# Two-layer f32 network, one core: stack constants by DMA, first passes before second passes, and short rounds spread over block 7

## The chip, the cores and the metric

The kernel runs on one core of a Trainium2 chip (trn2). The metric is the device time of one execution in microseconds (us), lower is better; the runs of the kernel before have a median of 3712.45 us.

## What is computed

The reference takes x (4 x 1024 x 128, f32) through two layers. Each layer is four steps of the form x = x + f(layernorm(x)): an attention, a mixture of experts, a second attention, a mixture of experts. Three pieces matter here.

The first attention of layer 0 has 16 heads of 8 values per sequence. Its scores are a causal table of distances (made from the mean of the inputs, through softmax, top-k and a sum of sines), plus one term for each query, one for each key, plus a small product of projected queries and keys:

```python
scores = jnp.take(causal_kern, jnp.maximum(doff, 0), axis=-1)
scores = scores + qm[..., :, None] + km[..., None, :]
scores = scores + MIX * jnp.einsum('bhic,bhjc->bhij', qc, kc) / math.sqrt(CR)
scores = jnp.where(causal, scores, -1000000000.0)
attn = jax.nn.softmax(scores, axis=-1)
```

The second attention of layer 1, the last attention of the network, has 16 heads of 64 values and one common key and value head:

```python
sim = jnp.einsum('bhid,bjd->bhij', q, k)
sim = sim + jnp.transpose(bias, (2, 0, 1))[None] * bias_scale
sim = jnp.where(causal_mask[None, None], -neg, sim)
attn = jax.nn.softmax(sim, axis=-1)
out = jnp.einsum('bhij,bjd->bhid', attn, v)
return out.transpose(0, 2, 1, 3).reshape(b, n, INNER) @ Wout + bout
```

## The kernel before

x stays in SBUF from start to end; the stages run one after another, each a block in which the five engines run programs of their own, coupled by semaphores. SyncE (SP) issues all DMAs.

**`l0a_project` (L1423, to about 119 us).** It normalizes x, transposes it and projects it to the dot parts of queries and keys, in eight groups g of 512 positions (batch b, half `par`). Each part is split into three bf16 pieces (`part["q"]`, `part["k"]`, `part["m"]`, two buffers by `par`) and SP sends them to DRAM (`send_parts` L1010 and L1484; `sent[par]`). ScalarE writes a buffer again two groups later and waits for `sent[par]` first (before L1567). Before the loop SP loads this stage's weights and those of the next mixture of experts (`load_l0_ffn`, L134).

**`l0a_table` (L1613).** It makes the distance table of the first attention. VectorE computes the mixing weights in a chain of small instructions on `l0at_gl`, `l0at_soft`, `l0at_hard` (L1732 to L1748); the sines and products follow from them. At the same time POOL prepares the stacks `l0a_qs` and `l0a_ks`: 128 rows x 3 stacks x 4 heads x 1024, bf16, 24 KB a row. A stack is what TensorE contracts over: rows 0 to 47 dot parts, 48 to 53 single terms and constants, from `MAX_ROWS` = 96 the rows of row maxima; all others have to be zero. POOL fills rows 32 to 63 and 64 to 127 with zeros (L1690, L1692), then SP, after `zeroed`, writes the constant rows (3 DMAs) and loads the dot parts (30 DMAs, `load_stack`, L1023 and L1025).

**`attention_two_pass` (from 277.9 to 874.2 us).** 64 heads in 16 quads. For a quad, `first_pass` (18 tiles t; L1191, L1198) computes scores by queries into `pP`, of which VectorE takes the minima (`low`, L1345); these go back as rows of the stack. `second_pass` (n, 36 units a quad, nine groups of four; L1228, L1231) computes the scores by keys into `pS`, a ring of three; ScalarE takes their exponential (L1317) and POOL multiplies it by the table (L1174), but for one unit in four (`ADDED`), where VectorE adds the table (L1339) and ScalarE takes the exponential after it (L1298). `weigh` (L1245) multiplies with the values. The first passes of a quad are issued `AHEAD` = 20 units before its second passes, one at every even n. The order on TensorE is that of the loop at L1259:

```python
for n in range(N):
    if n + RING - 1 < N:
        second_pass(n + RING - 1)
    if n % 2 == 0:
        quad, t = (n + AHEAD) // STEPS + 1, (n + AHEAD) % STEPS // 2
        if quad < QUADS:
            first_pass(quad, t)
```

**`attention_strips` (tag `l1ba`, from 2582 to 3447 us).** The last attention. A round r is 8 heads by one block of 128 queries; a group is the eight blocks 7, 6, ... 0 of one batch and one half of the heads, 64 rounds in 8 groups. The causal width is 128 keys for block 0, 1024 for block 7. A round is cut into units (one head each for blocks 7 to 4, two for 3 and 2, four for 1, eight for 0), numbered n; `FIRST[r]` is the first unit of round r. For each unit TensorE computes scores into `pS` (`scores`, L2463, or L2458 in block 0), VectorE adds the bias table `tab` and takes the minimum (`lows`, L2575), ScalarE the exponential (`exps`, L2523), VectorE, two units later, transposes in squares of 32 into `pT[r % 2]` (`turn`, L2584). `weigh` (L2483) multiplies the turned weights of a round with the values, spread over the units of the next round; ScalarE writes the result out (`out`, L2531) at `FIRST[r+2]+1`; POOL multiplies it by the inverse sums (`norm`, L2411), which SP brings from VectorE over DRAM (`spread_sums`); `project` (L2497) follows at `FIRST[r+3]+2`, and POOL adds it to x (L2419). POOL also copies the next group's far bias into `tab` (`fill`, L2426, semaphore `filled`) in the rounds of blocks 4 to 1. `turn` of round r waits with `pv_done` until round r − 2 has been weighed. SP loads the queries of round r + 2 at round r into `qs[:, r % 2]`, two DMAs a round.

## Time and profile before

| | us |
|---|---|
| median of three runs | 3712.45 (3709.52 to 3714.45) |
| the profiled execution | 3700.37 |
| its span | 3698.6 |
| TensorE busy | 3090.0 (84%) |
| VectorE busy | 2374.2 (64%) |
| ScalarE busy | 1844.5 (50%) |
| POOL busy | 1010.2 (27%) |

Busy time is the sum of an engine's instructions; weight loads of TensorE (PEld) are counted apart, since they overlap matmuls. A share over the whole span says little here, since each stage has its own limits; the stages are read one by one. "Idle before, releaser" in a row is how long the engine stood before an instruction, and which instruction's semaphore ended it. The clock column is the TensorE clock granted, 1.00 being 2.4 GHz and 0.50 being 1.2 GHz. The DMA share is the mean busy share of 16 DMA engines.

### The profile page before, as it was taken

What the parts mean: (1) busy time and instruction counts of PE and PEld (TensorE: products, weight loads), DVE (VectorE), ACT (ScalarE), POOL (GpSimd) and SP (SyncE); (2) the same over time, 40 slices, a digit from 0 to 9 for tenths busy, and PEclk for the clock granted to TensorE, in tenths of its full rate; (3) what the DMA queues carried; (4) which work ended last, traced back from release to release, by engine and by line L of the source; (5) the groups of instructions that cost most, each with busy time, mean ns of one, the idle gap of its engine ahead of it and who ended that gap; (6) DMA issues with size and microseconds to landing.
All of it is one profiled execution on the core that took longest, in us unless ns stands there. A gap on an engine that the chain in (4) does not pass through costs nothing. (4 is left out here: it accounts for less than half of the span.)

```text
span 3698.6 us, 67338 instructions
## 1 busy us (share of the span) xinstructions
PE 3090.0 (84%) x25109; PEld 1695.7 (46%) x25109; DVE 2374.2 (64%) x5080; ACT 1844.5 (50%) x3304; POOL 1010.2 (27%) x803
## 2 busy tenths in 40 slices
PE   5487777774859999797699978998989888999899
PEld 2123333331347555573222226764444544554676
DVE  5567777772856455564499953225988888888222
ACT  3115555553336323363289943433655565655344
POOL 1409888894100223000000000001222222222100
PEclk8679999997979899896599978999999999999999
DMA  4212232221032000132422210006524334322000
GB/s 136 86 60 75 75 109 77 98 79 33 13 120 115 1 1 1 47 130 83 143 64 65 68 47 10 1 9 220 107 73 102 90 95 99 90 80 71 27 10 12
DMA packets 214263, 260.64 MB, mean 70 GB/s; under 512 B 45213, under 2 KB 164473, under 8 KB 211622
## 3 DMA queue, kind: packets, MB, share of 16 engines
q1 hardware_dynamic: 213975, 256.78, 23.1%
q8 instruction: 183, 3.00, 0.3%
q14 instruction: 105, 0.86, 0.1%
HBM read 200.66 MB, written 56.55 MB: 70 GB/s over the span
## 5 line engine op out<-in xcount | busy, mean ns | idle before, releaser
L1174 POOL TENSOR_TENSOR l0aa_e<-l0aa_e,l0aa_et 128x512 f32<-128x512 f32 x432 | 535.7, 1275 | 97.8 <-ACT l0aa_e L1317 97.8
L2523 ACT ACTIVATE l1ba_sg<-l1ba_sg,l1ba_mn 128x128 f32<-128x128 f32 (+7 forms) x512 | 393.3, 769 | 243.4 <-DVE l1ba_mn L2575 242.3
L1345 DVE TENSOR_REDUCE l0aa_low<-l0aa_pP 128x8 f32<-128x1024 f32 x288 | 342.1, 1220 | 153.1 <-PE l0aa_pP L1198 152.3
L2575 DVE CUSTOM_DVE_ANT_0 l1ba_sg<-l1ba_pS,l1ba_tab 128x128 f32<-128x128 f32 (+7 forms) x512 | 368.8, 745 | 86.4 <-PE l1ba_pS L2463 64.2
L2584 DVE STREAM_TRANSPOSE l1ba_pT<-l1ba_sg 128x1024 f32<-128x1024 f32 (+3 forms) x344 | 367.1, 1067 | 37.1 <-PE l1ba_pO L2483 34.5
L319 PEld LDWEIGHTS f_pY<-l_w,f_hT 128*128 128x128 f32 x2048 | 268.1, 192 | 124.1 <-issue 118.8
L2483 PE MATMUL l1ba_pO<-l1ba_pT,l1ba_v 32*64 32x256 f32 x9216 | 314.8, 388 | 5.5 <-ACT l1ba_y L2538 4.6
L2411 POOL TENSOR_TENSOR l1ba_co<-l1ba_co,l1ba_rb 128x1024 f32<-128x1024 f32 x64 | 150.9, 2357 | 610.1 <-ACT l1ba_co L2531 545.4
L2940 ACT ACTIVATE l1aa_e<-l1aa_e 128x1536 f32<-128x1536 f32 x192 | 284.4, 1483 | 41.9 <-DVE l1aa_e L2981 25.3
L2463 PE MATMUL l1ba_pS<-l1b_k,l1ba_qs 64*128 64x384 f32 (+3 forms) x1024 | 262.2, 593 | 47.0 <-DVE l1ba_mn L2575 35.3
L1317 ACT ACTIVATE l0aa_e<-l0aa_pS 128x512 f32<-128x512 f32 x432 | 252.8, 592 | 82.1 <-PE l0aa_pS L1231 48.0
L282 ACT ACTIVATE f_hT<-f_pH,l_b 128x512 f32<-128x512 f32 x256 | 174.0, 687 | 237.3 <-PE f_pH L311 237.1
L1228 PE MATMUL l0aa_pS<-l0a_qs,l0a_ks 128*128 128x512 bf16 (+3 forms) x768 | 196.8, 330 | 107.9 <-DVE l0aa_e L1339 101.5
L319 PE MATMUL f_pY<-l_w,f_hT 128*128 128x128 f32 x2048 | 269.5, 275 | 2.4 <-ACT f_hT L282 2.4
L311 PE MATMUL f_pH<-f_xt,l_w 128*128 128x512 f32 x512 | 266.5, 604 | 0.0
L2483 PEld LDWEIGHTS l1ba_pO<-l1ba_pT,l1ba_v 32*64 32x64 f32 x9216 | 180.3, 132 | 165.1 <-issue 133.6
L2983 DVE SCALAR_TENSOR_TENSOR l1aa_e<-l1aa_pS,l1aa_ceiling 128x1536 f32<-128x1536 f32 x128 | 214.6, 1748 | 1.5 <-PE l1aa_pS L2900 1.4
L1191 PE MATMUL l0aa_pP<-l0a_ks,l0a_qs 96*128 96x512 bf16 (+3 forms) x768 | 184.7, 344 | 31.5 <-DMA l0aa_mask<-in_later_key 14.5
L2900 PE MATMUL l1aa_pS<-l1aa_qs,l1aa_ks 72*128 72x512 bf16 (+3 forms) x768 | 163.0, 336 | 52.0 <-DMA l1aa_ks<-l1a_kr 25.5
L590 PEld LDWEIGHTS f_pY<-l_w,f_hT 128*128 128x128 f32 x1152 | 151.8, 193 | 79.8 <-issue 65.0
L2497 PE MATMUL l1ba_pO<-l1ba_wo,l1ba_co 128*128 128x128 f32 x1024 | 135.9, 288 | 51.6 <-ACT l1ba_co L2531 44.7
L1228 PEld LDWEIGHTS l0aa_pS<-l0a_qs,l0a_ks 128*128 128x128 bf16 x768 | 62.6, 97 | 231.6 <-DVE l0aa_e L1339 195.0
(405 smaller groups left out, 5202.3 us busy)
## 6 DMA issues: line engine op xcount, KB each, us to landing
f_wB<-l0f_weights SPq DMA_DIRECT2D x16, 2048.0 KB, 7.2
l1ba_rb<-l1b_rdd SPq DMA_DIRECT2D x64, 512.0 KB
l0aa_et<-l0a_table SPq DMA_DIRECT2D x16, 1536.0 KB, 7.6
l1b_qd<-l1bp_part SPq DMA_DIRECT2D x64, 256.0 KB, 2.3
l1ba_qs<-l1b_qd SPq DMA_DIRECT2D x64, 256.0 KB
l0aa_et<-l0a_table SPq DMA_DIRECT2D x16, 512.0 KB, 8.1
l1ba_tab<-l1b_table SPq DMA_DIRECT2D x32, 256.0 KB, 5.2
l1ba_qs<-l1b_qd SPq DMA_DIRECT2D x64, 128.0 KB
```

The lines of the kernel that those rows point to most:

```text
L311: nc.tensor.matmul(pH[n % RING][:], w1[:, n % HT, :], xt[:, n // HT % 2, :], start=True, stop=True).then_inc(h_done, 1)
L319: ins = nc.tensor.matmul(pY[g % 2][:, k * P:(k + 1) * P], hT[:, n % RING, k * P:(k + 1) * P], w2[:, f, :], start=(f == 0 and k == 0), stop ...
L1174: nc.gpsimd.tensor_tensor(es, es, t, ALU.mult).then_inc(multiplied, 1)
L1228: ins = nc.tensor.matmul(pS[n % RING][:, at:at + w], ks[:, slot, j, kb * P:(kb + 1) * P], qs[:, slot, j, half * GROUP:half * GROUP + w], s ...
L1317: nc.scalar.activation(e[:, n % E_SLOTS, :], pS[n % RING][:], ACT.Exp, scale=-1.0).then_inc(e_done, 1)
L1345: nc.vector.tensor_reduce(low1[:, t, :], pP[TURN[quad, t]][:].rearrange("p (u t) -> p u t", t=P), AX.X, ALU.min).then_inc(p1_low, 1)
L2463: ins = nc.tensor.matmul(pS[n % 2][:, at:at + half], qs[lo:lo + HALF, r % 2, i, :], ks[lo:lo + HALF, key:key + half], start=True, stop=True)
L2483: ins = nc.tensor.matmul(pO[a][part * HALF:(part + 1) * HALF, 0:HG * Q], v4[a * Q:(a + 1) * Q, group_of(r)[0] % 2, (SEQ - width(r)) // Q + ...
L2523: nc.scalar.activation(row, row, ACT.Exp, bias=mn[:, r % 2, i + k:i + k + 1], scale=-1.0, accum_out=den[:, r % 2, i + k:i + k + 1]).then_i ...
L2575: nc.vector.tensor_tensor_reduce(row, scores, bias, 1.0, 3e38, ALU.add, ALU.min, mn[:, r % 2, h:h + 1]).then_inc(m_done, 1)
L2584: nc.vector.transpose(pT[r % 2][:, i * width(r):(i + heads) * width(r)], sg[:, n % RING, 0:heads * width(r)]).then_inc(t_done, 1)
L2940: nc.scalar.activation(es, es, ACT.Exp, scale=1 / ROOT).then_inc(e_done, 1)
```

## The change

Three parts, in three stages.

*Stack constants.* POOL's four fills and SP's wait for them go. A new function `fill_stacks` is issued by SP in `l0a_project`, behind `load_l0_ffn` and before the loop of sends. It loads rows of ones, minus ones and zeros from constants in DRAM, each broadcast twelvefold along a row, straight into the places: three loads of 3 rows, two of 42 rows (54 to 95), two of 29 rows (99 to 127). SP waits for all seven at the stage's end.

*First attention.* At even n the first pass is issued ahead of the second pass of unit n + 2.

*Last attention.* The turned weights of blocks 2, 1 and 0 go side by side into `pT1` (from columns 0, 3 x 1024 and 5 x 1024), those of other even blocks also there, odd ones in `pT0`; `turned_free` says which round's weighing has to be done before `turn` may write. Weighings of blocks 2, 1 and 0 move into block 7's eight units of the next group (units 0 to 2, 3 and 4, 5 and 6), the projections of blocks 3, 2 and 1 to its units 3, 5 and 7. `out` stands at the last step of a weighing, ahead of that unit's exponentials. Block 7's queries get a place of their own (`q7`, columns 6 x 1024 to 7 x 1024 of `pT1`) and a semaphore, and are loaded at block 3 of the group before.

```diff
@@ -1257,12 +1257,12 @@
             for n in range(RING - 1):
                 second_pass(n)
             for n in range(N):
-                if n + RING - 1 < N:
-                    second_pass(n + RING - 1)
                 if n % 2 == 0:
                     quad, t = (n + AHEAD) // STEPS + 1, (n + AHEAD) % STEPS // 2
                     if quad < QUADS:
                         first_pass(quad, t)
+                if n + RING - 1 < N:
+                    second_pass(n + RING - 1)
...
-def l0a_project(nc, D, x, C, tag, h0, v_all, pooled, qd, kd, qm, km):
+STACK_CONSTANTS = 7
+
+
+def fill_stacks(sp, D, qs, ks, ready):
+
+    for dst, name in ((qs[51:54], "minus_ones"), (ks[48:51], "ones"), (ks[MAX_ROWS:MAX_ROWS + 3], "ones"),
+                      (qs[54:MAX_ROWS], "zeros"), (qs[MAX_ROWS + 3:], "zeros"), (ks[54:MAX_ROWS], "zeros"), (ks[MAX_ROWS + 3:], "zeros")):
+        rows = dst.shape[0]
+        sp.dma_start(dst.rearrange("p s j t -> p (s j) t"), D[name][0:rows].unsqueeze(1).broadcast_to([rows, STACKS * 4, SEQ])).then_inc(ready, 16)
+
+
+def l0a_project(nc, D, x, C, tag, h0, v_all, pooled, qd, kd, qm, km, qs, ks):
...
             load_l0_ffn(sp, D, C)
+            fill_stacks(sp, D, qs, ks, filled)
             for b in range(BATCH):
...
+            sp.wait_ge(filled, 16 * STACK_CONSTANTS)
...
-            sp.wait_ge(zeroed, 4)
-            for dst, src in ((qs[51:54], "minus_ones"), (ks[48:51], "ones"), (ks[MAX_ROWS:MAX_ROWS + 3], "ones")):
-                sp.dma_start(dst.rearrange("p s j t -> p (s j) t"), D[src].unsqueeze(1).broadcast_to([3, STACKS * 4, SEQ])).then_inc(stacks_in, 16)
...
-            sp.wait_ge(stacks_in, 16 * (3 + STACKS * STACK_LOADS))
+            sp.wait_ge(stacks_in, 16 * STACKS * STACK_LOADS)
...
             nc.gpsimd.memset(L[:], 0.0).then_inc(zero, 1)
-            pool.wait_ge(zero, 1)
-            for i, stack in enumerate((qs, ks)):
-                nc.gpsimd.memset(stack[32:64], 0.0).then_inc(zeroed, 1)
-                pool.wait_ge(zeroed, 2 * i + 1)
-                nc.gpsimd.memset(stack[64:P], 0.0).then_inc(zeroed, 1)
-                pool.wait_ge(zeroed, 2 * i + 2)
...
+    END = N + 9
+
+    def turned(r):
+
+        return {2: (1, 0), 1: (1, 3 * HG * P), 0: (1, 5 * HG * P)}.get(block_of(r), (1 - block_of(r) % 2, 0))
+
+    def turned_free(r):
+
+        return r - {7: 3, 6: 1, 1: 2, 0: 5}.get(block_of(r), 1)
+
+    def next_group(r):
+
+        return FIRST[r + block_of(r) + 1]
+
+    def weigh_steps(r):
+
+        if block_of(r) <= 2:
+            at, steps = {2: (0, 3), 1: (3, 2), 0: (5, 2)}[block_of(r)]
+            return next_group(r) + at, steps
+        return FIRST[r + 1] + 3, FIRST[r + 2] - FIRST[r + 1] - 1
+
+    def out_step(r):
+        first, steps = weigh_steps(r)
+        return first + steps - 1
+
+    def project_step(r):
+        if 1 <= block_of(r) <= 3:
+            return next_group(r) + {3: 3, 2: 5, 1: 7}[block_of(r)]
+        return FIRST[r + 3] + 2 if r + 1 < ROUNDS else N + 8
     def pairs(r):
...
         pT = [sb("pT0", [P, HG * SEQ]), sb("pT1", [P, HG * (SEQ - P)])]
+        q7 = pT[1][:, 6 * HG * P:7 * HG * P].rearrange("p (h q) -> p h q", q=P)
...
             def load_queries(r):
-                if r >= 2:
-                    sp.wait_ge(s_done, FIRST[r - 1])
+                slot = block_of(r) % 2
+                if block_of(r) == U - 1:
+                    if r >= U:
+                        sp.wait_ge(pv_done, r - U + 2)
+                    dst, done = q7, q7_in
+                else:
+                    before = {6: 2, 5: 4}.get(block_of(r), 2)
+                    if r >= U or block_of(r) < 5:
+                        sp.wait_ge(s_done, FIRST[r - before + 1])
+                    dst, done = qs[:, slot], q_in[slot]
                 b, hg = group_of(r)
                 row, col = (b * 2 + hg) * HG * HD, block_of(r) * P
                 rows = qd[row:row + HG * HD, col:col + P]
                 if paired(r):
                     for i in (0, 2):
-                        sp.dma_start(qs[:, r % 2, i:i + 2], rows[i * P:(i + 2) * P, :].rearrange("(k p) q -> p k q", p=P)).then_inc(q_in[r % 2], 16)
+                        sp.dma_start(dst[:, i:i + 2], rows[i * P:(i + 2) * P, :].rearrange("(k p) q -> p k q", p=P)).then_inc(done, 16)
                 else:
                     for lo in (0, HALF):
-                        sp.dma_start(qs[lo:lo + HALF, r % 2], rows.rearrange("(h d) q -> d h q", d=HD)).then_inc(q_in[r % 2], 16)
+                        sp.dma_start(dst[lo:lo + HALF], rows.rearrange("(h d) q -> d h q", d=HD)).then_inc(done, 16)
             def load_values(b):
                 if b >= 2:
@@ -2388,8 +2434,10 @@
                 u = block_of(r)
                 if r and u > 1:
                     spread_sums(r - 1)
-                if r + 2 < ROUNDS:
+                if r + 2 < ROUNDS and block_of(r + 2) != U - 1:
                     load_queries(r + 2)
+                if u == 3 and r + 4 < ROUNDS:
+                    load_queries(r + 4)
...
                 b, half = group_of(r)[0], width(r) // 2
-                if i == 0:
-                    pe.wait_ge(q_in[r % 2], 32 * (r // 2 + 1))
+                slot = block_of(r) % 2
+                queries = q7 if block_of(r) == U - 1 else qs[:, slot]
+                if i == 0 and block_of(r) == U - 1:
+                    pe.wait_ge(q7_in, 32 * (r // U + 1))
+                elif i == 0:
+                    pe.wait_ge(q_in[slot], 32 * (r // U * (4, 3)[slot] + (U - block_of(r)) // 2))
...
-                rows = pT[r % 2][:, 0:HG * width(r)].rearrange("p (h w) -> p h w", w=width(r))
+                tile, c = turned(r)
+                rows = pT[tile][:, c:c + HG * width(r)].rearrange("p (h w) -> p h w", w=width(r))
                 for s in range(lo, hi):
                     for a in range(STRIPS):
                         for part in (0, 1):
...
-            for n in range(FIRST[ROUNDS + 2] + 3):
+            for n in range(END):
                 if n < N:
                     scores(n)
                 for r in range(ROUNDS):
-                    if n == FIRST[r + 3] + 2:
+                    if n == project_step(r):
                         project(r)
                 for r in range(ROUNDS):
-                    first, units = FIRST[r + 1] + 2, FIRST[r + 2] - FIRST[r + 1]
-                    if units > 1:
-                        first, units = first + 1, units - 1
+                    first, units = weigh_steps(r)
                     if first <= n < first + units:
...
-            for n in range(FIRST[ROUNDS + 2] + 3):
+            for n in range(END):
                 for r in range(ROUNDS):
-                    if n == FIRST[r + 3] + 2:
+                    if n == project_step(r):
                         projected(r)
+                for r in range(ROUNDS):
+                    if n == out_step(r):
+                        out(r)
                 if n < N:
                     exps(n)
-                for r in range(ROUNDS):
-                    if n == FIRST[r + 2] + 1:
-                        out(r)
         @block.vector
...
                 if r >= 2 and i == 0:
-                    dve.wait_ge(pv_done, r - 1)
-                nc.vector.transpose(pT[r % 2][:, i * width(r):(i + heads) * width(r)], sg[:, n % RING, 0:heads * width(r)]).then_inc(t_done, 1)
+                    dve.wait_ge(pv_done, turned_free(r))
+                tile, c = turned(r)
+                nc.vector.transpose(pT[tile][:, c + i * width(r):c + (i + heads) * width(r)], sg[:, n % RING, 0:heads * width(r)]).then_inc(t_done, 1)
```

On SP, in `l0a_project`, the place between the last load of the experts' constants (`l_rank`) and the first send. Before:

```order
L134 DMA l_rank<-in_rank 128x8
L1010 DMA l0a_qd<-l0ap_partq 128x3x512
L1010 DMA l0a_qd<-l0ap_partq 128x2x512
L1010 DMA l0a_qd<-l0ap_partq 128x512
L1010 DMA l0a_kd<-l0ap_partk 128x3x512
```

And now:

```order
L134 DMA l_rank<-in_rank 128x8
L1431 DMA l0a_qs<-in_minus_ones 3x12x1024
L1431 DMA l0a_ks<-in_ones 3x12x1024 x2
L1431 DMA l0a_qs<-in_zeros 42x12x1024
L1431 DMA l0a_qs<-in_zeros 29x12x1024
L1431 DMA l0a_ks<-in_zeros 42x12x1024
L1431 DMA l0a_ks<-in_zeros 29x12x1024
L1010 DMA l0a_qd<-l0ap_partq 128x3x512
```

Seven loads, two of them with 29 rows, now stand ahead of every send in the same queue.

On TensorE, in the first attention, around a weighing (`pO`) with `pS` the second passes, `pP` the first. Before:

```order
L1191 MATMUL l0aa_pP<-l0a_ks,l0a_qs 128x512 x2
L1198 MATMUL l0aa_pP<-l0aa_mask,ident 128x128 x2
L1228 MATMUL l0aa_pS<-l0a_qs,l0a_ks 128x512
L1231 MATMUL l0aa_pS<-l0aa_mask,ident 128x128
L1245 MATMUL l0aa_pO<-l0aa_e,l0aa_vh 32x512 x4
L1228 MATMUL l0aa_pS<-l0a_qs,l0a_ks 128x512
L1231 MATMUL l0aa_pS<-l0aa_mask,ident 128x128
L1191 MATMUL l0aa_pP<-l0a_ks,l0a_qs 128x512 x2
```

And now:

```order
L1198 MATMUL l0aa_pP<-l0aa_mask,ident 128x128 x2
L1228 MATMUL l0aa_pS<-l0a_qs,l0a_ks 128x512
L1231 MATMUL l0aa_pS<-l0aa_mask,ident 128x128
L1228 MATMUL l0aa_pS<-l0a_qs,l0a_ks 128x512
L1231 MATMUL l0aa_pS<-l0aa_mask,ident 128x128
L1245 MATMUL l0aa_pO<-l0aa_e,l0aa_vh 32x512 x4
L1191 MATMUL l0aa_pP<-l0a_ks,l0a_qs 128x512 x2
L1198 MATMUL l0aa_pP<-l0aa_mask,ident 128x128
```

The first pass comes directly behind the weighing, and two second passes stand together.

On ScalarE, in the last attention, the eight units of block 7 (exponentials of width 1024) and the first of block 6 (896); `co<-pO` is `out`, `y<-pO` the copy of a projection. Before:

```order
L2523 ACTIVATE l1ba_sg,l1ba_den<-l1ba_sg,l1ba_mn 128x1024
L2531 ACTIVATE l1ba_co<-l1ba_pO 128x8x32 x4
L2538 ACTIVATE l1ba_y<-l1ba_pO 128x128
L2523 ACTIVATE l1ba_sg,l1ba_den<-l1ba_sg,l1ba_mn 128x1024 x6
L2523 ACTIVATE l1ba_sg,l1ba_den<-l1ba_sg,l1ba_mn 128x896 x2
L2531 ACTIVATE l1ba_co<-l1ba_pO 128x8x32 x4
```

And now:

```order
L2574 ACTIVATE l1ba_sg,l1ba_den<-l1ba_sg,l1ba_mn 128x1024
L2589 ACTIVATE l1ba_y<-l1ba_pO 128x128
L2574 ACTIVATE l1ba_sg,l1ba_den<-l1ba_sg,l1ba_mn 128x1024
L2582 ACTIVATE l1ba_co<-l1ba_pO 128x8x32 x4
L2574 ACTIVATE l1ba_sg,l1ba_den<-l1ba_sg,l1ba_mn 128x1024
L2589 ACTIVATE l1ba_y<-l1ba_pO 128x128
L2574 ACTIVATE l1ba_sg,l1ba_den<-l1ba_sg,l1ba_mn 128x1024
L2574 ACTIVATE l1ba_sg,l1ba_den<-l1ba_sg,l1ba_mn 128x896 x8
L2574 ACTIVATE l1ba_sg,l1ba_den<-l1ba_sg,l1ba_mn 128x768
L2582 ACTIVATE l1ba_co<-l1ba_pO 128x8x32 x4
```

Outs and projections of the short blocks now alternate with the last units of block 7, none is left in block 6, and the out of block 7 comes after one exponential of width 768.

## Rows read from the trace of the kernel before

**Rows 1.** POOL's timeline at the fills (start, duration, instruction), first and last of four.
```profile
120.49 10.33 POOL L1690 MEMSET l0a_qs<- 32x12288 bf16 x1
...
151.66 10.33 POOL L1692 MEMSET l0a_ks<- 64x12288 bf16 x1
```

**Rows 2.** VectorE's timeline in the same stretch.
```profile
141.92 9.72 DVE L1739 TENSOR_SCALAR l0at_soft<-l0at_soft,l0at_two 64x16 f32<-64x16 f32 x1
...
151.88 10.15 DVE L1742 TENSOR_SCALAR l0at_hard<-l0at_soft,l0at_top 64x16 f32<-64x16 f32 x1
...
162.62 0.23 DVE L1746 TENSOR_SCALAR l0at_hard<-l0at_hard,l0at_two 64x16 f32<-64x16 f32 x1
```

**Rows 3.** Windows: length, busy PE, PEld, DVE, ACT, POOL, clock, DMA share, GB/s.
```profile
277.90:874.20 596.30, 463.16 (x3746) 208.71 (x3744) 421.09 (x555) 350.49 (x648) 535.67 (x432) 1.00 0.25 80
...
840.00:874.20 34.20, 21.38 (x176) 7.27 (x168) 6.23 (x9) 20.42 (x37) 34.20 (x28) 0.96 0.03 6
```

**Rows 4.** Waits from 300 to 870 us: total, times, longest.
```profile
POOL l0aa_e L1174 <- ACT l0aa_e L1317: 60.6, 98, 2.3
```

**Rows 5.** Timeline of the first attention, one cycle; idle time before in brackets.
```profile
504.80 2.36 DVE L1345 TENSOR_REDUCE l0aa_low<-l0aa_pP 128x8 f32<-128x1024 f32 x2 [1.03 <-PE l0aa_pP L1198]
...
507.07 0.68 DVE L1339 TENSOR_TENSOR l0aa_e<-l0aa_pS,l0aa_et 128x512 f32<-128x512 f32 x1
...
508.03 0.60 PE L1191 MATMUL l0aa_pP<-l0a_ks,l0a_qs 96*128 96x512 bf16 x3
```

**Rows 6.** The last attention as one window, columns as in rows 3.
```profile
2582.00:3447.00 865.00, 768.80 (x11776) 425.59 (x11776) 720.85 (x1496) 506.97 (x1344) 232.94 (x190) 0.96 0.35 90
```

**Rows 7.** VectorE's timeline from block 7's first turn to block 6.
```profile
2788.64 1.25 DVE L2584 STREAM_TRANSPOSE l1ba_pT<-l1ba_sg 128x1024 f32<-128x1024 f32 x1 [1.61 <-PE l1ba_pO L2483]
...
2794.19 1.25 DVE L2584 STREAM_TRANSPOSE l1ba_pT<-l1ba_sg 128x1024 f32<-128x1024 f32 x1 [2.64 <-PE l1ba_pO L2483]
...
2798.84 1.22 DVE L2575 CUSTOM_DVE_ANT_0 l1ba_sg<-l1ba_pS,l1ba_tab 128x1024 f32<-128x1024 f32 x1 [1.13 <-PE l1ba_pS L2463]
...
2801.16 1.18 DVE L2575 CUSTOM_DVE_ANT_0 l1ba_sg<-l1ba_pS,l1ba_tab 128x1024 f32<-128x1024 f32 x1
...
2810.28 1.05 DVE L2575 CUSTOM_DVE_ANT_0 l1ba_sg<-l1ba_pS,l1ba_tab 128x896 f32<-128x896 f32 x1
...
2818.64 1.09 DVE L2575 CUSTOM_DVE_ANT_0 l1ba_sg<-l1ba_pS,l1ba_tab 128x896 f32<-128x896 f32 x1 [1.57 <-PE l1ba_pS L2463]
```

**Rows 8.** TensorE's timeline: scores, projection, weighing; then two projections that wait.
```profile
2788.39 1.13 PE L2463 MATMUL l1ba_pS<-l1b_k,l1ba_qs 64*128 64x512 f32 x4
2789.56 2.02 PE L2497 MATMUL l1ba_pO<-l1ba_wo,l1ba_co 128*128 128x128 f32 x16
2792.04 1.99 PE L2483 MATMUL l1ba_pO<-l1ba_pT,l1ba_v 32*64 32x256 f32 x64 [0.46 <-ACT l1ba_y L2538]
...
2833.96 2.02 PE L2497 MATMUL l1ba_pO<-l1ba_wo,l1ba_co 128*128 128x128 f32 x16 [0.81 <-ACT l1ba_co L2531]
...
2866.97 2.02 PE L2497 MATMUL l1ba_pO<-l1ba_wo,l1ba_co 128*128 128x128 f32 x16 [1.00 <-ACT l1ba_co L2531]
```

**Rows 9.** SP's timeline: the last load of constants, and the first send.
```profile
23.50 0.43 SPq L134 DMA_DIRECT2D l_rank<-in_rank  x1
37.64 1.56 SPq L1010 DMA_DIRECT2D l0a_qd<-l0ap_partq  x3
```

**Rows 10.** Windows as rows 3: weight loads, sends, stack loads, 68-row loads.
```profile
24.00:26.00 2.00, 2.00 (x10) 2.00 (x10) 1.09 (x9) 0.00 (x0) 1.32 (x2) 1.00 0.89 189
40.00:42.00 2.00, 2.00 (x3) 0.18 (x1) 0.68 (x5) 0.00 (x0) 1.01 (x1) 0.50 1.03 341
...
170.00:172.00 2.00, 2.00 (x3) 0.23 (x1) 1.24 (x2) 0.69 (x1) 0.00 (x0) 0.50 0.35 121
...
1699.00:1700.00 1.00, 0.00 (x0) 0.00 (x0) 0.00 (x0) 0.00 (x0) 0.00 (x0) 0.50 0.30 123
```

**Rows 11.** ScalarE's timeline: the third group of the projection.
```profile
55.66 0.60 ACT L1567 ACTIVATE l0ap_partq<-l0ap_pQ 128x512 bf16<-128x512 f32 x1 [5.72 <-PE l0ap_pQ L1603]
```

12 lines of the change are left out of this document (6 added, 6 removed).

## The prediction

> **What bounds the kernel now.** I read the page first: one core, so there is no skew between cores to look for. Then, for each of the three stages that the diff touches, the busy times by stage, the waits, and the timeline of the engine that is waited for.
>
> *Stage one, the constants of the stacks.* POOL fills four row ranges with zeros, unbroken from 120.49 to 162 [rows 1]. In the same stretch VectorE has a chain of instructions on 64x16 elements, and two of them last 9.72 and 10.15 us, each ending within 0.1 us of the end of a fill [rows 1, 2]; a like one, right after the last fill, takes 0.23 us [rows 2]. VectorE is what the stage waits for there: the mixing weights come out of this chain, and TensorE and the rest of the table follow it. So the fills cost time though no semaphore says so.
>
> *Stage two, the first attention.* Of 596.3 us POOL is busy 535.7, TensorE 463.2, VectorE 421.1, ScalarE 350.5 [rows 3]. There are 16 quads of nine groups of four units, 144 groups, so a group costs POOL 3.72 us, TensorE 3.22, VectorE 2.92, ScalarE 2.43, and takes 596.3 / 144 = 4.14. POOL has the most work but isn't unbroken: it waits 60.6 us for ScalarE's exponentials [rows 4]. Behind that stands a loop: VectorE's two low reductions take 2.36 us from 504.80, its addition comes at 507.07 (0.68 us), TensorE then issues the second pass that needs the addition, and only after it the first pass (from 508.03) whose tile the next low reduction waits 1.03 us for [rows 5]. The last quad, where no first pass is left, shows the floor: POOL 34.20 us of 34.20 [rows 3].
>
> *Stage three, the last attention.* Of 865 us TensorE is busy 768.8 and VectorE 720.9 [rows 6]. Both are close to the span, and which waits last changes from round to round. In the change from one group of eight rounds to the next, VectorE waits 1.61 and 2.64 us for the weighing that frees its tile of turned weights, then 1.13 us for scores [rows 7]. In three later rounds of the group TensorE stands 0.81 to 1.00 us before a projection, until ScalarE has written out a weighed block; the first and the last of the three are shown [rows 8].
>
> **The change part by part.**
>
> *Constants: gain.* The fills by POOL go. The two long instructions fall to the 0.23 us of their like: 9.49 + 9.92 = **−19 us**. The lower end is the gain gone (0), if something other than the fills makes them long; that each ends with a fill speaks against it, so I take the whole. SP's wait for the fills goes too, and its stack loads start some 26 us earlier; they are worth nothing, since SP waits after them for the table.
>
> *Constants: cost.* In place of the fills SP issues seven loads, between its last weight load at 23.50 and the first sends at 37.64 [rows 9]. A row is 12 x 1024 bf16 = 24,576 bytes; 3+3+3+42+29+42+29 = 151 rows are 3.7 MB. Issuing is free: SP is idle there. What counts is over how many engines a load is spread. The sends, from 128 rows, use them all: share 1.03, 341 GB/s, so 341 / (1.03 x 16) = 20.7 GB/s for one engine. The loads of two 68-row tiles, which stand alone at 1699 to 1700, run at a share of 0.30 and 123 GB/s, 4.8 engines of 16 and 25.6 GB/s each; the stack loads, whose source lies in six pieces, at 0.35 and 121 GB/s, 5.6 engines [rows 10]. 68 = 4 x 17 and 6 are what these look like: equal shares of whole rows, as many engines as divide them. By that 42 rows go over 14 engines, three rows go over 3, and **29, a prime, over one**. The first engine then gets 3 x 1 + 2 x 3 + 2 x 29 = 67 rows, 1.647 MB: at 25.6 GB/s 64 us, from about 26 to 90; at 20.7 GB/s 80 us, to 106. The sends of the first group have a sixteenth of 1.67 MB (104 KB, 5 us) on this engine, and if an engine takes its work in order they land at about 95 instead of before 50. ScalarE's third group, which overwrites the buffer that they read, starts at 55.66 [rows 11]; it would start at 95: **+40 us**, with everything of the stage behind it. TensorE already runs at 0.50 of its clock in this stretch [rows 10], so standing costs it no clock. Ends: 0 (spread over all 16 engines: 3.7 MB at 341 GB/s, 11 us, done before 37.64), and the rate of the weight loads at 24 to 26, 189 / (0.89 x 16) = 13.3 GB/s [rows 10]: 124 us, the third group at 155, +100. I take the like loads' rate, and +30 to +60 for the range.
>
> The Trainium skill speaks against this part: its page "DMA: Bandwidth & Descriptors", section "Why a DMA increments its semaphore by 16 and not by 1", has it that a transfer uses the largest number of engines, at most 16, that divides the slowest dimension of both sides. The rows at 68 and six agree (they show 4.8 and 5.6 where it gives 4 and 6). By its rule the 29-row loads have one engine, as in my sum; without it, by spreading evenly, the sum would be 40 us less.
>
> *Order of the first attention.* The first pass now stands before the second pass that needs the addition, so the tile for the low reductions is written while the addition runs. The loop is then 2.36 + 0.68 and some 0.1 to 0.3 of hand-over, 3.1 to 3.4 us, under POOL's 3.72. What is late next is POOL: the gain is its waits, 60.6 us, less what is not of this loop (quad boundaries, where rows are rewritten and POOL's next product waits): I leave 5. **−55 us**, ends −60 and −40 (TensorE at 3.22 us of 3.72 has only 0.5 us to spare, and any wait of it comes back once in 4 steps). The moved pass delays each second pass by its own time, 0.5 to 0.7 us; the ring of three keeps that from POOL.
>
> *Last attention.* VectorE's turned weights of blocks 2, 1 and 0 get places of their own, so it no longer waits for the weighing of the blocks before; the weighing and projections go into block 7's eight units. VectorE's unit there is 2.28 us long ((2810.28 − 2801.16) / 4 [rows 7]). TensorE has scores (1.06 net of the overlap), a weighing of 32 (1.0, half of 1.99) or 16 matmuls (about 0.6), a projection (2.0) [rows 8]: from the fourth to the eighth unit 4.1 + 2.1 + 3.65 + 1.7 + 3.05 = 14.6 us against VectorE's 11.4. TensorE is 3.2 us behind, of which the units it is ahead cover about 1.8: 1.4 us of wait is left. There is a new wait too: POOL norms and fills the table of the next group in one queue. The norm of block 1 now stands behind a weighing that comes later, and the fill of the last two heads behind it: I work out 1.4 us late at block 6. So of 1.61 + 2.64 + 1.13 = 5.4 us, and 0.2 before the first unit, 2.8 stay: −2.8 at each of seven changes. In block 6 the projection of block 1 is gone, and with it VectorE's 1.57 us wait [rows 7]: −1.6 seven times. ScalarE's writing out now comes before the exponentials of its unit, an exponential earlier, so TensorE's three waits of 0.81 to 1.00 us go [rows 8]: some 2.6 us for each of eight groups. 7 x 4.4 + 8 x 2.6 = **−52 us**. Ends −30 (the new fill wait twice as long, half of the projection waits stay) and −75 (no fill wait, and others of TensorE's waits for ScalarE go too). The queries of block 7 are the same two loads, sent earlier; SP now waits for other semaphores before them, all long met. The first round and the last rounds' chain of sums, norm and projection stay as they are: 0.
>
> **Sum.** 3700.4 (the profiled execution) − 19 + 40 − 55 − 52 = 3614. The runs' median stands 12 us above the profiled execution, so I forecast 3614 + 12 = **3626 us**, 86 below the median of before.
>
> **The rivals.**
> 1. *The zero loads don't hold the sends.* If they are spread over the engines, or engines take turns between transfers, +40 becomes 0: 3586. For it: no row shows a prime number of rows. Against: neither the 68-row nor the six-piece loads were spread. Chance 0.10.
> 2. *The first attention gives half.* TensorE or a quad boundary is the next bound instead of POOL: −25 instead of −55, 3656. For it: TensorE needs 3.22 of 3.72 us a group, with waits of its own. Against: the last quad's unbroken POOL. 0.12.
> 3. *The last attention gives little.* POOL's queue (norm, then add, then fill) becomes the bound at each change of groups: a wait of 6 us there, seven times, leaves −15 of −52: 3663. POOL's norm already waits for its sums there, and only 4.4 us of slack is counted on. 0.08.
> 4. *Slower: the single engine.* Gains are 19 + 55 + 52 = 126 us. The change is slower by over 0.2% when the third group starts over 134 us late, at 190, so when 1.647 MB take over 159 us, under 10.4 GB/s. The nearest rows have 20.7 and 25.6, the slowest 13.3. At 9 GB/s it would be 183 us, start 214, +158: 3744. Between 10.4 and 11.4 GB/s it is a draw. 0.06: draw 0.02, slower 0.04.
>
> **The numbers.** The forecast's own case has 0.64. About 0.2% of the time, 7.4 us, is what a measurement of this kernel can tell from no change. Faster: 0.64 + 0.10 + 0.12 + 0.08 = 0.94. The range reaches down to 3580 (rival 1, and a last attention at −58) and up to 3665 (rivals 2 and 3, and +60 for the loads with some of the gain short); what lies beyond is rival 4 and pairs of shortfalls.
>
> **What would show it.** Right: ScalarE's third group in the projection starts near 95 after a wait for a DMA, with a DMA share near 0.06 from 50 to 90; the two VectorE instructions take 0.2 us; the first attention lasts about 540 us with POOL busy 535; the last attention about 813 us, waits of VectorE for the weighing gone, a wait for `filled` (POOL) of 1 to 2 us at block 6. Wrong: a projection stage that still ends near 119 (rival 1); POOL's waits for ScalarE above 25 us (rival 2); a last attention above 840 us (rival 3).

## The result, and the profile after

The changed kernel takes **3677.2 us** (median of 7 runs, 3667.3 to 3691.2) against 3710.8 us of the kernel before (7 runs): ratio 0.991, 95% interval 0.9897 to 0.9924. It is 0.9% faster, where 2.3% was forecast, and the median lies 12 us above the range. The profiled execution has a span of 3675.4 us against 3698.6: 23.2 us less. By stages (start of the table stage, POOL's first and last product, first scores and last addition of the last attention):

| stage | before, us | after, us | difference | forecast |
|---|---|---|---|---|
| up to the table stage (projection) | 119.5 | 171.2 | +51.7 | +40 |
| table stage | 118.2 | 98.4 | −19.8 | −19 |
| first attention, POOL's products | 596.3 | 598.7 | **+2.4** | **−55** |
| last attention | 864.6 | 799.2 | −65.4 | −52 |
| all between | 2000.0 | 2007.9 | +7.9 | 0 |

Three of four terms have the right sign and roughly the right size; the 55 us of the first attention are missing whole. The last line is code that the change doesn't touch. In it 6.9 of the 7.9 us lie in the first attention of layer 1, which took 351.2 us at a mean granted clock of 0.93, and 344.3 at 0.95 before. Over the traces of all twelve kernels shown here this line goes from 1993.6 to 2010.3 us, so 7.9 is within what comes without a change.

**Projection.** SP's timeline (start, duration, instruction), from the first constant on, and ScalarE's third group, the row that answers to [rows 11]:

```profile
24.35 0.31 SPq L1431 DMA_DIRECT2D l0a_qs<-in_minus_ones  x1
...
26.87 37.97 SPq L1431 DMA_DIRECT2D l0a_ks<-in_zeros  x2
64.88 29.16 SPq L1010 DMA_DIRECT2D l0a_qd<-l0ap_partq  x1
```

```profile
107.38 0.60 ACT L1580 ACTIVATE l0ap_partq<-l0ap_pQ 128x512 bf16<-128x512 f32 x1 [56.66 <-DMA l0a_km<-l0ap_partm]
```

Before, SP took under 1.5 us for each DMA of this stage; now the last two zero loads together (42 and 29 rows) take 38 us and the first send takes 29. I read this as SP being held until there is room in the queue of the one engine that has work. The DMA columns of the windows show what the queue is doing (columns as in [rows 3]: the last two are the share of 16 engines and GB/s):

```profile
34.00:38.00 4.00, 3.47 (x23) 2.57 (x21) 2.95 (x6) 2.92 (x6) 0.00 (x0) 1.00 0.27 72
...
46.00:56.00 10.00, 6.47 (x23) 2.69 (x21) 7.32 (x26) 3.01 (x7) 1.62 (x2) 0.83 0.07 25
...
58.00:62.00 4.00, 0.15 (x2) 0.00 (x0) 0.00 (x0) 0.00 (x0) 0.00 (x0) 0.79 0.92 181
...
70.00:92.00 22.00, 0.00 (x0) 0.00 (x0) 0.00 (x0) 0.00 (x0) 0.00 (x0) 0.50 0.07 25
...
104.00:107.00 3.00, 0.00 (x0) 0.00 (x0) 0.00 (x0) 0.00 (x0) 0.00 (x0) 0.50 1.02 341
```

0.07 of 16 is one engine, and it moves 25 GB/s: the 29-row loads have a single engine, at the rate that I took from the 68-row loads. The burst from about 57 to 63 moves some 1.0 MB, the size of the second load of 42 rows (42 x 24,576 bytes). So, as I read it, most of SP's 38 us passed before that load could go out. Behind the constants, at 104, the sends take all engines again.

**Table stage.** VectorE's two long instructions of [rows 2] are short:

```profile
193.39 0.23 DVE L1743 TENSOR_SCALAR l0at_soft<-l0at_soft,l0at_two 64x16 f32<-64x16 f32 x1
...
193.85 0.23 DVE L1746 TENSOR_SCALAR l0at_hard<-l0at_soft,l0at_top 64x16 f32<-64x16 f32 x1
```

**First attention.** The stage as one window, then POOL's timeline over one quad and a bit:

```profile
309.70:908.35 598.65, 487.40 (x3746) 220.06 (x3743) 485.84 (x555) 346.16 (x648) 532.67 (x432) 0.94 0.25 79
```

```profile
341.47 1.26 POOL L1174 TENSOR_TENSOR l0aa_e<-l0aa_e,l0aa_et 128x512 f32<-128x512 f32 x1 [3.47 <-ACT l0aa_e L1317]
343.60 2.50 POOL L1174 TENSOR_TENSOR l0aa_e<-l0aa_e,l0aa_et 128x512 f32<-128x512 f32 x2 [0.87 <-ACT l0aa_e L1317]
346.27 29.54 POOL L1174 TENSOR_TENSOR l0aa_e<-l0aa_e,l0aa_et 128x512 f32<-128x512 f32 x24 [0.17 <-ACT l0aa_e L1317]
379.28 1.26 POOL L1174 TENSOR_TENSOR l0aa_e<-l0aa_e,l0aa_et 128x512 f32<-128x512 f32 x1 [3.47 <-ACT l0aa_e L1317]
```

Before, POOL's timeline had runs of three products with gaps between them for half of a quad, and a run of twelve:

```profile
303.93 3.77 POOL L1174 TENSOR_TENSOR l0aa_e<-l0aa_e,l0aa_et 128x512 f32<-128x512 f32 x3 [0.46 <-ACT l0aa_e L1317]
...
316.49 3.73 POOL L1174 TENSOR_TENSOR l0aa_e<-l0aa_e,l0aa_et 128x512 f32<-128x512 f32 x3 [0.32 <-ACT l0aa_e L1317]
321.47 14.81 POOL L1174 TENSOR_TENSOR l0aa_e<-l0aa_e,l0aa_et 128x512 f32<-128x512 f32 x12 [1.25 <-ACT l0aa_e L1317]
```

Now it makes 24 without a gap. But once a quad it stands 3.47 and 0.87 us (65.5 us in all from 330 to 870, as much as the 60.6 of [rows 4]), and from 341.47 to 379.28 the quad takes 37.8 us, as before (37.7). What it stands for begins on VectorE, in the same stretch. VectorE's timeline, then TensorE's, then the window right behind, with the clock in its third column from the end:

```profile
371.13 4.83 DVE L1372 TENSOR_TENSOR l0aa_mp<-l0aa_rest,l0aa_mp 32x128 bf16<-32x128 f32 x1
...
375.88 1.21 DVE L1345 TENSOR_REDUCE l0aa_low<-l0aa_pP 128x8 f32<-128x1024 f32 x1
```

```profile
377.75 0.61 PE L1228 MATMUL l0aa_pS<-l0a_qs,l0a_ks 128*128 128x256 bf16 x2 [4.45 <-DVE l0aa_e L1339]
```

```profile
379.00:381.00 2.00, 2.00 (x11) 1.18 (x9) 0.90 (x1) 0.46 (x2) 1.26 (x1) 0.50 0.00 0
```

A subtraction on 32x128 elements lasts 4.83 us and ends at 375.96, 0.15 us after POOL's run of products (346.27 + 29.54 = 375.81). VectorE's addition comes behind it, so TensorE stands 4.45 us for the addition, and no new exponentials reach POOL. Then something follows that the kernel before didn't have: behind this stand of TensorE its granted clock falls to 0.50 (1.2 GHz) for 3 to 7 us, once a quad. The stage's mean is 0.94 (first row above), against 1.00 in [rows 3]. How much of POOL's 4.3 us is the wait itself and how much the slow clock behind it, no run here separates; without the wait both go (e2, e3).

This is the subtraction's spread over 16 quads (duration in ns, least, median, most), first before, then after:

```profile
L1372 DVE TENSOR_TENSOR l0aa_mp<-l0aa_rest,l0aa_mp x16: 278/466/8449, 267.3 to 825.4; 32x128 bf16<-32x128 f32 x16
```

```profile
L1372 DVE TENSOR_TENSOR l0aa_mp<-l0aa_rest,l0aa_mp x16: 280/4837/10208, 299.1 to 857.5; 32x128 bf16<-32x128 f32 x16
```

It isn't a gap of POOL that the subtraction used before. There it started at 304.88, while POOL was at the first product of a run (303.93 to 305.20), and ended at 305.34, 0.14 us after that product, with the second product right behind. What differs in the traces is whether POOL's next product is ready, that is, whether ScalarE's exponential for it has ended. Before, then after:

```profile
304.28 0.60 ACT L1317 ACTIVATE l0aa_e<-l0aa_pS 128x512 f32<-128x512 f32 x1 [0.43 <-PE l0aa_pS L1231]
...
304.88 0.47 DVE L1372 TENSOR_TENSOR l0aa_mp<-l0aa_rest,l0aa_mp 32x128 bf16<-32x128 f32 x1
```

```profile
370.25 0.60 ACT L1317 ACTIVATE l0aa_e<-l0aa_pS 128x512 f32<-128x512 f32 x1
```

Before, the exponential ended at 304.88, as the subtraction started; so it was in fourteen quads, and the subtraction waited for one product. After, it had ended at 370.85, 0.27 us ahead of the subtraction (371.13); three more products went first, although two of them became ready only later, and then POOL had no more. That the readiness decides it is my reading of these times; no run changes it alone. All fifteen subtractions that met products after the change ended 0.13 to 0.15 us after the last product of a run.

**Last attention.** Waits of VectorE, then of TensorE, there, after the change (total, times, longest):

```profile
DVE l1ba_sg L2626 <- PE l1ba_pS L2515: 28.9, 33, 7.9
DVE l1ba_pT L2636 <- ACT l1ba_sg L2574: 12.8, 32, 1.6
...
DVE l1ba_pT L2636 <- PE l1ba_pO L2536: 5.4, 8, 0.8
DVE l1ba_sg L2626 <- POOL l1ba_tab L2474: 2.6, 2, 2.2
```

```profile
PE l1ba_pO L2550 <- ACT l1ba_co L2582: 4.8, 9, 0.6
```

And the same waits before, VectorE's first, then TensorE's:

```profile
DVE l1ba_sg L2575 <- PE l1ba_pS L2463: 64.2, 50, 7.9
DVE l1ba_pT L2584 <- PE l1ba_pO L2483: 34.5, 22, 2.7
```

```profile
PE l1ba_pO L2497 <- ACT l1ba_co L2531: 44.7, 41, 3.6
```

### The profile page after: what moved, and what is told of

It reads as the page before. It is cut to its first block and busy times, and to the rows that moved or that the text cites. A ratio compares the mean times of both kernels' runs of the same rounds, so it can differ in the third digit from the quotient of the medians.

```text
span 3675.4 us, 67297 instructions
## 1 busy us (share of the span) xinstructions
PE 3107.7 (85%) x25109; PEld 1698.9 (46%) x25109; DVE 2416.6 (66%) x5080; ACT 1839.0 (50%) x3304; POOL 966.2 (26%) x799
## 5 line engine op out<-in xcount | busy, mean ns | idle before, releaser
L1317 ACT ACTIVATE l0aa_e<-l0aa_pS 128x512 f32<-128x512 f32 x432 | 243.9, 593 | 113.0 <-PE l0aa_pS L1231 75.9
L319 PE MATMUL f_pY<-l_w,f_hT 128*128 128x128 f32 x2048 | 269.6, 275 | 2.7 <-ACT f_hT L282 2.7
L1191 PE MATMUL l0aa_pP<-l0a_ks,l0a_qs 96*128 96x512 bf16 (+3 forms) x768 | 192.9, 357 | 30.7 <-DMA l0aa_mask<-in_later_key 14.5
L2515 PE MATMUL l1ba_pS<-l1b_k,l1ba_qs 64*128 64x448 f32 (+2 forms) x768 | 178.6, 546 | 18.4 <-DVE l1ba_mn L2626 18.4
L590 PEld LDWEIGHTS f_pY<-l_w,f_hT 128*128 128x128 f32 x1152 | 151.9, 194 | 79.7 <-issue 64.9
L1245 PE MATMUL l0aa_pO<-l0aa_e,l0aa_vh 128*32 128x512 f32 (+3 forms) x1536 | 157.8, 507 | 11.9 <-POOL l0aa_e L1174 11.9
L590 PE MATMUL f_pY<-l_w,f_hT 128*128 128x128 f32 x1152 | 152.4, 277 | 11.6 <-DVE f_hT L458 11.6
```

The lines of the kernel that those rows point to most:

```text
L319: ins = nc.tensor.matmul(pY[g % 2][:, k * P:(k + 1) * P], hT[:, n % RING, k * P:(k + 1) * P], w2[:, f, :], start=(f == 0 and k == 0), stop ...
L590: ins = nc.tensor.matmul(pY[g % 2][:, k * P:(k + 1) * P], hT[:, n % RING, k * P:(k + 1) * P], w2[:, f, :], start=(f == 0 and k == 0), stop ...
L1317: nc.scalar.activation(e[:, n % E_SLOTS, :], pS[n % RING][:], ACT.Exp, scale=-1.0).then_inc(e_done, 1)
```

## The experiments

After the profile I held two theories. **Constants:** a load of 29 rows, a prime number above 16, has one DMA engine, and both SP and the sends wait for it. **First attention:** VectorE's subtraction can't start while POOL is at a product; the new order took away the gaps between POOL's products in which it used to slip in (by the times above: the ends of products with no other ready behind them), so it now lasts until POOL runs out of work, which it does because VectorE stands. Their rivals were the bytes as such, and some other boundary of the quad, like the rows' way over DRAM.

**e1_rows28.** Each load of 29 rows is cut in two; the bytes stay.

```diff
-STACK_CONSTANTS = 7
+STACK_CONSTANTS = 9
...
-(qs[MAX_ROWS + 3:], "zeros"), (ks[54:MAX_ROWS], "zeros"), (ks[MAX_ROWS + 3:], "zeros")
+(qs[MAX_ROWS + 3:P - 1], "zeros"), (qs[P - 1:], "zeros"), (ks[54:MAX_ROWS], "zeros"),
+(ks[MAX_ROWS + 3:P - 1], "zeros"), (ks[P - 1:], "zeros")
```

> Changed kernel, but each load of 29 zero rows is cut into one of 28 rows and one of one row; same bytes. Theory (one DMA engine carries a load with a prime number of rows, and everything sent later in the queue waits for it): the first engine gets 3 + 6 + 4 + 2 = 15 rows instead of 67, SP issues without a stall, ScalarE's third group starts near 56 instead of 107.4, the stage ends near 120 instead of 171.2, total some 50 us below the changed kernel: about 3627. Rival (it is the 3.7 MB or the number of their pieces that SP stalls on, wherever they go): same stall, same 3677. Rival (the loads are late in any case, since the weight loads before them fill the engines): half of it, about 3650.

3632.0 us, ratio 0.9791 (0.9775 to 0.9807). The same bytes, with one row split off two loads, and the medians are 3677.2 − 3632.0 = 45 us apart. The table stage starts at 122.6 instead of 171.2, and from 40 to 50 us all engines are busy (share 0.96), not one:

```profile
40.00:50.00 10.00, 6.15 (x28) 3.44 (x28) 8.59 (x31) 3.96 (x8) 1.62 (x2) 0.93 0.96 170
```

SP is still held for about 10 us twice, so ScalarE's third group starts at 59.0, 3 us late, not at 56. That much is due to the bytes, wherever they go; for the other 48 us the rivals fall.

**e2_low_on_pool.** The subtraction moves to POOL, in its queue of products. VectorE, before it writes the subtraction's input again a quad later, now waits for POOL.

```diff
+            def remainder_low(quad):
+                pool.wait_ge(mid_ready, quad + 1)
+                nc.gpsimd.tensor_tensor(mp[:, quad % 2, 2, :], rest[:], mp[:, quad % 2, 1, :], ALU.subtract).then_inc(rows_ready, 1)
+
+            remainder_low(0)
...
+                if n % STEPS == STEPS - AHEAD + 7 and n // STEPS + 1 < QUADS:
+                    remainder_low(n // STEPS + 1)
...
+                if quad:
+                    dve.wait_ge(rows_ready, quad)
...
-                if after == 8 and more:
-                    remainder_low(n // STEPS + 1)
```

> Changed kernel, but the subtraction that makes the third part of the row maxima (VectorE, 32x128, both inputs in SBUF, once a quad) is made by POOL, ahead of its unit 23 of a quad. Theory (in the changed kernel POOL multiplies without a gap, and this VectorE instruction cannot start while POOL is at it: it takes 4.8 us instead of 0.5, and POOL then runs dry for 3.5 + 0.9 us): both go, the first attention takes 596.3 - 14 x 3.5 or about 545 us instead of 598.7, total near 3625. Rival (the rest of a quad's boundary, the rows' way over DRAM and back, sets 37.7 us a quad whatever engine subtracts): the first attention stays within 5 us of 598, total 3677. POOL itself pays 0.3 us a quad, 5 us in all.

3616.1 us, ratio 0.9748 (0.9731 to 0.9764), 61 us below the changed kernel. POOL's timeline and the stage's window:

```profile
365.81 0.42 POOL L1172 TENSOR_TENSOR l0aa_mp<-l0aa_rest,l0aa_mp 32x128 bf16<-32x128 f32 x1
366.19 33.24 POOL L1182 TENSOR_TENSOR l0aa_e<-l0aa_e,l0aa_et 128x512 f32<-128x512 f32 x27
```

```profile
310.10:847.00 536.90, 459.61 (x3746) 207.89 (x3743) 407.21 (x540) 348.86 (x648) 536.90 (x447) 1.00 0.27 89
```

POOL is busy 536.90 us of 536.90. The stage is 59.4 us shorter than before, nearly the whole of the 60.6 us of waits in [rows 4], and the clock is at 1.00 throughout.

**e3_gap.** The subtraction stays on VectorE, in its place, with its inputs; POOL waits for it once a quad.

```diff
             for n in range(N):
                 g, j = n // QUAD, n % QUAD
+                if n % STEPS == STEPS - AHEAD + 8 and n // STEPS + 1 < QUADS:
+                    pool.wait_ge(rows_ready, n // STEPS + 2)
```

> Changed kernel, but POOL waits for that subtraction once a quad, ahead of its unit 24; the instruction stays on VectorE with the same inputs and the same place. Theory (lock): with POOL standing still the subtraction takes under 0.6 us, and POOL loses that and a hand-over, about 1 us a quad, instead of 4.3: the first attention takes about 550 to 560 us, total near 3635. Rival (it is slow because of its own operands or place, or a boundary of the quad is the bound): it still takes 4.8 us, and the wait adds to the time: above 3677.

3616.9 us, ratio 0.9746 (0.9712 to 0.9781): **a wait was added, and the kernel is 60 us faster.** With POOL standing for 0.27 us, the subtraction takes 269 ns:

```profile
L1374 DVE TENSOR_TENSOR l0aa_mp<-l0aa_rest,l0aa_mp x16: 268/269/5092, 308.9 to 807.2; 32x128 bf16<-32x128 f32 x16
```

```profile
376.29 24.64 POOL L1176 TENSOR_TENSOR l0aa_e<-l0aa_e,l0aa_et 128x512 f32<-128x512 f32 x20 [0.27 <-DVE l0aa_mp L1374]
```

The stage takes 537.0 us, as in e2, and less than the 550 to 560 that I had expected. Neither the instruction's operands nor its place nor the way over DRAM made it slow, only that POOL always had a product to go on with.

**e4_both.** The edits of e1 and e2 together.

> Both edits of e1 and e2. The two stages don't touch each other, so the gains add if the theories hold: 3677 - 50 - 52 = about 3575, 3.7% below the kernel before. If either rival holds, 3625 or 3677.

3568.4 us, ratio **0.9614 (0.9591 to 0.9636)**. Of the sum expected (3575) 7 us better; table stage at 122.5, products 537.1, last attention 805.8. This is the version to keep; it beats both kernels.

**e5_only_order.** The kernel before with the new order of passes alone.

> Kernel before with the new order of first and second passes alone. Theory (gain inside a quad, given back at its end by the subtraction that waits for POOL): the first attention takes 598 to 600 us against 596.3, total within 4 us of the kernel before, about 3710. Rival (in the changed kernel it was the later start or the other two parts that ate this gain): 537 to 545 us and about 3655.

3714.0 us, ratio 1.0015 (1.0000 to 1.0029): no gain. The products take 598.8 us at a mean clock of 0.94, and the subtraction has the same spread, both as in the changed kernel:

```profile
L1372 DVE TENSOR_TENSOR l0aa_mp<-l0aa_rest,l0aa_mp x16: 280/4866/10277, 265.9 to 824.4; 32x128 bf16<-32x128 f32 x16
```

**e6_only_strips.** The kernel before with the new last attention alone.

> Kernel before with the new last attention alone. Theory (that stage stands for itself): it takes 799 to 807 us against 864.6, total about 3708 - 61 = 3647. Rival (part of the 65 us seen there is the clock, which was granted higher in that execution): the stage takes 820 or more, total above 3665.

3634.3 us, ratio 0.9799 (0.9779 to 0.9819), so 73 us between the medians; the stage takes 804.0 us, 60.6 less than before. The stage's gain stands for itself. The rest of the 73 isn't in the stage: the two profiled spans are 64.9 us apart (3698.6 and 3633.7), 60.6 of them in the stage, and the profiled execution of the kernel before lies 7 us under the median that it is compared with here. The wait for POOL's filling of the table, which I had foreseen, is there:

```profile
DVE l1ba_sg L2622 <- POOL l1ba_tab L2470: 11.1, 8, 1.8
```

8 times, 1.4 us each: what I had worked out for a change of groups. In the changed kernel it came twice.

**e7_no_constants.** As e4, but the constants filled by POOL as in the kernel before.

> Kernel before with the new order, the new last attention and the subtraction on POOL (as in e2), but with the constants filled by POOL as before: e4 without its first part. Theory: projection stage ends at 119.5 (e4: 122.5), the table stage takes 118 us with the two long VectorE instructions back (e4: 109.5), so 6 us above e4, up to 17 if e4's table stage gets its clock early: 3574 to 3585. Rival (the fills cost nothing, since the clock would have been low anyway): same as e4 or 3 us below.

3577.1 us, ratio 0.9647 (0.9625 to 0.9669): 9 us above e4, within what was expected, but the intervals overlap, and the two profiled spans are only 0.7 us apart. In the traces the first product comes at 284.8 here and at 272.1 in e4; the table stage takes 125.6 us here, 109.5 in e4. So loading the constants well is worth some 13 us at most, and a gain in the total isn't shown.

**e8_out_late.** e4 with ScalarE's writing out after the exponentials of its unit, as it was before.

```diff
-                for r in range(ROUNDS):
-                    if n == out_step(r):
-                        out(r)
                 if n < N:
                     exps(n)
+                for r in range(ROUNDS):
+                    if n == out_step(r):
+                        out(r)
```

> Kernel e4, but in the last attention ScalarE writes a weighed block out after the exponentials of its unit, not before. By my sum this order is worth three waits of TensorE a group, 2.6 us, 8 times: the stage takes 21 us more (805.8 to 827), total near 3589. Rival (the moved weighings and projections make the gain; the order is covered by VectorE): within 5 us of e4. If it costs more than 40 us, the order carries most of the stage's gain.

3642.1 us, ratio 0.9838 (0.9813 to 0.9863). The stage takes 876.7 us: 71 more than in e4, and **12 more than before the change**. (In e5, whose last attention is the code of before, it took 872.1 us, so only the 71 is far beyond what comes without a change.) My 21 us were far too few. TensorE's wait for ScalarE before projections is larger than it ever was, and VectorE waits for scores and for the fill:

```profile
PE l1ba_pO L2554 <- ACT l1ba_co L2586: 67.0, 53, 2.8
```

```profile
DVE l1ba_sg L2630 <- PE l1ba_pS L2519: 80.8, 45, 8.0
DVE l1ba_sg L2630 <- POOL l1ba_tab L2478: 19.0, 7, 2.7
```

**e9_out_first_only.** e4 with the last attention of the kernel before, and only the order of `out` and `exps` changed in it.

> Kernel e4 with the last attention of the kernel before, in which only one thing is changed: ScalarE writes a weighed block out ahead of the exponentials of that unit. e8 showed that without this order the spread schedule takes 876.7 us, not 805.8. Theory A (the order by itself carries the gain, the spreading adds little): the stage takes 805 to 815, total near 3570 to 3580. Theory B (the two need each other: the order only removes the three waits a group of my sum, the spreading its two): 840 to 850, total near 3607. Theory C (no gain from the order without the spreading): 865, total near 3627.

3594.2 us, ratio 0.9698 (0.9679 to 0.9718); the stage takes 829.6 us. That lies between theories A and B:

```profile
PE l1ba_pO L2505 <- ACT l1ba_co L2539: 3.2, 5, 0.8
```

```profile
DVE l1ba_pT L2592 <- PE l1ba_pO L2491: 34.9, 22, 3.4
DVE l1ba_sg L2583 <- PE l1ba_pS L2471: 30.7, 39, 7.9
```

So the stage has four corners: 864.6 with neither (872.1 in e5), 829.6 with the order alone (−35), 876.7 with the spreading alone (+12), 805.8 with both (−59). The order takes away TensorE's waits for ScalarE and half of VectorE's for scores. The spreading takes away VectorE's waits for its tile (34.9 to 5.3 us), and is only worth that once the order is right. With the late order TensorE waits before 53 projections, not 41; why that takes back the whole gain I only infer from these waits.

**e10_fills_later.** e4 with the constants' loads behind the second group's sends.

> Kernel e4 with the loads of the constants issued after the second group's sends instead of ahead of the first. Theory (in order on each DMA engine): in e4 the sends of the first group wait for 3.7 MB, SP stalls some 20 us in all and the projection stage ends at 122.5; here no send is waited for at that point, the stage ends at 119 to 120: 3 us less than e4, about 3565, which the total can hardly show. If the sends of the third group are now late, the stage ends at 123 or later.

3571.8 us, ratio 0.9635 (0.9617 to 0.9654), the same as e4. The stage didn't get shorter but longer: the table stage starts at 131.0, not at 119. The 3.7 MB now lie in the way of the third group's sends:

```profile
62.66 11.29 SPq L1010 DMA_DIRECT2D l0a_qd<-l0ap_partq  x3
```

For this stage they are better ahead of the first sends (122.5 in e4); the totals don't tell the two apart, since the table stage took 98.8 us here and 109.5 in e4. My expectation named this outcome but not as the likely one.

## Why the prediction was wrong

- **First attention, the step that failed:** "the gain is its waits, 60.6 us, less what is not of this loop (quad boundaries ...): I leave 5". The loop inside the quad came out as worked out: POOL runs unbroken, and with the subtraction out of the way the stage is 59 us shorter (e2, e3). The overlap that failed is that of VectorE with POOL: once a quad a wait of about 4.3 us appeared that was not there before (POOL's 3.47 + 0.87; with 15 quads some 65 us, where 5 were left). In the traces this short VectorE instruction gets in where POOL's next product isn't ready, and the change made it ready; behind each such wait TensorE's clock was at 0.50 as well. Rival 2 had the size in part (−25) but named other causes, TensorE or the boundary as such; its sign, POOL's waits above 25 us, came (65.5).
- The evidence was in my own rows: [rows 1, 2] show VectorE instructions that end when POOL's fills end, and I used them for the gain of the constants; I didn't ask which VectorE instructions would meet a POOL that I was about to make busy without a break. The spread of the subtraction before the change says it too: 466 ns at the median and 8449 at the most. The long one is the last, from 825.42 to 833.87, in a run of products that ends at 833.73. In e3 the last one is again the long one (5092 ns): VectorE came to it early, when POOL still had three products to make before its wait.
- **Constants, cost:** +40 against +51.7. The mechanism is as predicted, one engine at 25 GB/s (shown by the windows, and by e1, where it goes). The term that was mis-sized is its start: I let the engine begin at 26, but up to 34 most engines were still at work (share 0.72 from 26 to 30, 0.90 from 30 to 34), and only from 38 on is it one alone. 67 rows at 25 GB/s are 66 us, so by this estimate 38 + 66 = 104, not 90. "Issuing is free" was wrong too: SP was held for 38 us and then for 29, until 94, so the sends that I had waiting on the engine were not even issued. The last of them lands at about 107, when ScalarE goes on.
- **Constants, gain:** −19 against −19.8, right in this execution. In e1 and e4 the same stage took 109.5 us, not 98.4; TensorE, which the stage waits for once the chain is done, had a lower mean clock there (0.70 against 0.79), so against the 118.2 us of before the gain is 9 to 20 us by when the clock rises. With POOL's fills the stage varies too; it took 125.6 us in e7.
- **Last attention:** −52 against −65.4 (−58 to −64 in the other traces of the same code), in its range. Its parts were mis-sized in both directions: the order of `out` and `exps` alone gives 35 us, not 21, and the spreading gives 24 on top of it and nothing without it. The waits before projections were counted three times a group; the waits view had 41 of them, 44.7 us, and that line should have bounded the term.
- **Elsewhere:** 0 against +7.9, in unchanged code, within the spread of this line over the traces. That the errors of the constants' cost (+11.7) and of the last attention (−13.4) nearly cancel is luck.
- **Range and rivals:** 3677 lies outside 3580 to 3665. The sum of the forecast with rival 2 at zero gain instead of −25 would have been 3681. No rival let the whole gain of a part come back as a new wait.

The sum with what the runs showed: 3700.4 + 51.7 − 19.8 + 2.4 − 65.4 + 7.9 = 3677.2, the time of the profiled execution after.

## What to carry to other kernels

When a change makes POOL busy without a gap, look at every VectorE instruction of that stretch for its spread of durations, not its mean: one that is short at the median and long at the most may be waiting for POOL, and then it can wait for a whole run of products. Compare the end of the long one with the ends of POOL's instructions. Two remedies did equally well here (3616.1 and 3616.9 us): the instruction on POOL itself (0.42 us), or one deliberate wait of POOL for it (0.3 us, for 4.3 saved). Before a transfer is put ahead of others in a queue, factor its number of rows: one row split off 29 was worth 45 us. And a part of a change can be worth nothing without another: the spreading over units gave 24 us with the new order on ScalarE, and none without it. So undo the parts one by one before deciding what made the gain.
